# Two transformer-like blocks on one core: order of ropes, stores, norm turns and rotation tables, and where the bias sums are made

## The reference, cut to what matters

```python
xn = layernorm(x)                                    # layer 0
s = attention(xn, 32 heads of 16, rope, causal) @ out_w + out_b
g = silu((silu(xn @ W_gate.T) * (xn @ W_up.T)) @ W_down.T)
x = x + s * g
xn = layernorm(x)                                    # layer 1
h = xn @ Win.T + bin                                 # the "chain", 64 features
for l in range(4):
    y = silu(layernorm(h) * ln1_w[l] + ln1_b[l])
    h = h + sc_lin[l] * Re(complex recurrence of y)  # h_t = p * h_{t-1} + y_t
    y = layernorm(h) * ln2_w[l] + ln2_b[l]
    h = h + silu(y @ W1[l].T + b1[l]) @ W2[l].T + b2[l]
s = (layernorm(h) * lnl_w + lnl_b) @ Wout.T + bout
g = silu(octonion_ffn(xn, ternary(w_gate), ternary(w_up), ternary(w_down)))
x = x + s * g
```

## Time and profile before

| | |
|---|---|
| timed runs | 674.81 us median (671.32, 674.81, 674.85) |
| profiled execution | 678.76 us, its span 677.0 us |
| busy share of the span | PE 92%, DVE 55%, POOL 54%, ACT 41% |
| mean granted PE clock | 0.975 of full speed |
| DMA | 83.24 MB, 123 GB/s mean |

### The profile page before, as it was taken

The page is one execution under the profiler, slowest core; times in us unless marked ns, Lnnn a source line. Parts: engine busy times, 40 slices in busy tenths (PEclk is TensorE's granted clock), DMA queues, the critical chain, the costliest instruction groups (busy, mean ns, idle before and its releaser), DMA issues.

```text
span 677.0 us, 9849 instructions
## 1 busy us (share of the span) xinstructions
PE 621.6 (92%) x3372; PEld 428.2 (63%) x3372; DVE 375.6 (55%) x916; ACT 276.1 (41%) x439; POOL 368.9 (54%) x591
## 2 busy tenths in 40 slices
PE   2978899999999997879999999999999978999996
PEld 2856565666567785546656665677887545757654
DVE  4949668666245592765775653358645240426165
ACT  3514455555634522244555555343122332232323
POOL 4767656555333744865565545347841486730264
PEclk9999999999999999898999999999799987999999
DMA  8687856654312326787575544724500000000002
GB/s 283 185 282 223 254 140 178 179 133 101 119 47 78 88 78 179 208 282 206 127 217 135 132 100 155 274 70 148 187 0 1 1 0 1 0 1 0 1 32 93
DMA packets 59889, 83.24 MB, mean 123 GB/s; under 512 B 17840, under 2 KB 26288, under 8 KB 59840
## 3 DMA queue, kind: packets, MB, share of 16 engines
q1 hardware_dynamic: 56192, 71.35, 36.7%
q10 hardware_dynamic: 3648, 11.27, 4.5%
HBM read 64.78 MB, written 26.99 MB: 136 GB/s over the span
## 4 chain that ended last, share of the span: by engine, by line
PE 72%; DVE 9%; DMA 6%; POOL 5%; issue 3%; ACT 2%; SPq 2%; ACTq 1%; DVEq 0%; POOLq 0%
PE proj_ps L896 8%; PE ctx_ps L1054 6%; PE proj_ps L898 5%; PE proj_ps L897 5%; PE score_ps L926 4%; PE proj_ps L1102 3%; PE proj_ps L1103 3%; PE scoreT_ps L935 3%; DMA rows<-rows_lo 3%; PE score_ps L896 2%; PE score_ps L898 2%; PE score_ps L897 2%; PE scoreT_ps L896 2%; PE scoreT_ps L898 2%; PE scoreT_ps L897 2%
## 5 line engine op out<-in xcount | busy, mean ns | idle before, releaser
L723 POOL TENSOR_TENSOR w_lo<-raw,w_hi 128x512 fp32r<-128x512 f32 x98 | 131.1, 1342 | 71.8 <-ACT w_hi L1253 65.2
L1432 DVE CUSTOM_DVE_ANT_0 score_ps<-score_ps,causal 128x512 f32<-128x512 f32 (+3 forms) x256 | 120.0, 517 | 67.7 <-PE score_ps L926 67.2
L1300 ACT ACTIVATE probs_T<-scoreT_ps 128x1024 f32<-128x1024 f32 (+1 forms) x96 | 84.8, 884 | 83.4 <-PE scoreT_ps L935 82.7
L896 PE MATMUL proj_ps<-xn_hi,w_hi 128*128 128x512 f32 x224 | 101.0, 451 | 5.1 <-DVE gate_silu L1471 2.7
L897 PE MATMUL proj_ps<-xn_hi,w_lo 128*128 128x512 f32 x224 | 89.2, 398 | 0.0
L898 PE MATMUL proj_ps<-xn_lo,w_hi 128*128 128x512 f32 x224 | 89.1, 398 | 0.0
L721 POOL TENSOR_SCALAR w_hi<-raw 128x512 fp32r<-128x512 f32 x50 | 31.1, 621 | 59.2 <-PE proj_ps L898 44.2
L896 PEld LDWEIGHTS proj_ps<-xn_hi,w_hi 128*128 128x128 f32 x224 | 42.5, 190 | 30.4 <-issue 13.5
L926 PE MATMUL score_ps<-k_st,q_st 50*128 50x512 f32 (+3 forms) x256 | 45.1, 389 | 13.8 <-DVE row_max L1432 8.4
L926 PEld LDWEIGHTS score_ps<-k_st,q_st 50*128 50x128 f32 x256 | 21.9, 186 | 54.9 <-issue 28.0
L757 POOL TENSOR_SCALAR_AFFINE_SELECT probs_T<-probs_T 128x256 f32<-128x256 f32 x128 | 50.5, 415 | 10.9 <-ACT probs_T L1300 10.9
(11 more groups left out here) (301 smaller groups left out, 1318.0 us busy)
## 6 DMA issues: line engine op xcount, KB each, us to landing
raw<-w SPq DMA_DIRECT2D x98, 256.0 KB, 2.9
rows<-rows_hi SPq DMA_DIRECT2D x32, 256.0 KB, 3.9
arranged<-tern SPq DMA_DIRECT2D x96, 85.0 KB
q_st<-rows SPq DMA_DIRECT2D x32, 200.0 KB
k_st<-rows SPq DMA_DIRECT2D x32, 200.0 KB
rows<-rows_lo SPq DMA_DIRECT2D x16, 256.0 KB, 4.3
gate_w<-arranged ACTq DMA_DIRECT2D x4, 704.0 KB, 7.1
up_w<-arranged ACTq DMA_DIRECT2D x4, 704.0 KB, 8.0
```

The lines of the kernel that those rows point to most:

```text
L723: nc.gpsimd.tensor_tensor(w_lo[n % SPLIT][:, :], raw[n % RAW][:, :], F32(w_hi[n % SPLIT][:, :]), ALU.subtract).then_inc(unit_ready, 1)
L896: nc.tensor.matmul(acc, lh, rh, start=first, stop=False)
L1300: nc.scalar.activation(probs_T[gp % 4][:, c:c + 2 * w].rearrange("p (h c) -> p h c", h=2), scoreT_ps[:, :, 0:w], ACT.Exp, scale=0.25).then ...
L1432: m = nc.vector.tensor_tensor_reduce(out=block, in0=block, in1=causal[:, S - w:], scale=1.0, scalar=-3e38, op0=ALU.add, op1=ALU.max, accum ...
```

## The change

- Table l lies in buffer l % 3 instead of l % 2. Table 2 enters `todo` at spread(0) and table 3 at conv(2), and a doubling is put only beside an item for whose successor four further on (`AHEAD`) no `hsL` is made. Table 2 waits until the input projection is done, table 3 for layer 0's recurrence. By the list, table 2 is then built beside items 24 to 38 (before: 38 to 52) and table 3 beside items 62 to 76 (before: 60 to 74).
- The running sums of bin and b2 are made by five small POOL operations ahead of table 0, and one product of five columns centres them. W1 times ln2_b is a product and a reduction on DVE in `chain_weights`, on two tensors that SP loads with `winR`.
- DVE does the four rope calls of the next batch between products and residual sums.
- At the head of a batch SP loads 12 units instead of 10, writes the rotated rows after load 9 instead of ahead of it, and reads stack 0 after load 11.
- The six stores of ternary weights are issued by SP in slot 1 of batch 0.
- X is stored tile by tile in slots 24 to 27 of batch 1, and x loaded over it in slots 32 to 35.
- The norm turns 0 and 1 stay in slot 60, and 2 and 3 go to slot 61, on PE, ACT and DVE.

```diff
@@ -142,6 +142,10 @@
+def turns_in(s):
+    return {NORM_TURN: (0, 1), NORM_TURN + 1: (2, 3)}.get(s, ())
+
+
 def turn_order():
@@ -150,9 +154,8 @@
             at["max", max_in(s)] = len(at)
-        if s == NORM_TURN:
-            for kc in range(KC):
-                at["xn", kc] = len(at)
+        for kc in turns_in(s):
+            at["xn", kc] = len(at)
         if s == LAST_DOWN:
@@ -176,7 +179,7 @@
 HI_BY_ACT = FILL + 3
-RAW_HEAD = 10
+RAW_HEAD = 12
 RAW, SPLIT = 4, 5
@@ -187,6 +190,7 @@
+X_OUT, X_BACK = (24, 25, 26, 27), (32, 33, 34, 35)
 W_GATE, W_UP, W_DOWN = range(3)
@@ -353,7 +358,7 @@
     w2T = sb("w2T", [P, DEPTH, 2, C1], f32, offset=o_pt + 22528 + 4096)
-    rotation = [sb(f"rotation{n}", [P, 2, S], f32, offset=o_ctx + 4096 * n) for n in range(2)]
+    rotation = [sb(f"rotation{n}", [P, 2, S], f32, offset=(o_ctx, o_ctx + 4096, o_work + 18432)[n]) for n in range(3)]
     xm_hi = sb("xm_hi", [P, KC, S], f32r, offset=o_v)
@@ -668,11 +678,16 @@
                         write_edges(0)
-                    if u == 8:
+                    if u == 9:
                         write_rows(b, Q_UNIT[0])
                         write_rows(b, K_UNIT[0])
-                        read_rows(b, 0)
+                read_rows(b, 0)
                 for s in range(SCORE_SLOTS + 1):
+                    if b == 0 and s == 1:
+                        for w in range(3):
+                            sp.wait_ge(wp_ready, w + 1)
+                            for x, src in enumerate((tern_pos[w], tern_neg[w])):
+                                sp.dma_start(tern_d[w][x].rearrange("(p n) -> p n", p=P), F32(src[:, :])).then_inc(tern_stored, 16)
                     for u in written_in(s):
@@ -685,19 +700,22 @@
                         sp.dma_start(*copies.pop(0)).then_inc(arranged, 16)
-                    if b == 1 and s == 2:
-                        sp.wait_ge(combined, 2 * NT)
-                        sp.dma_start(x2_d[0].rearrange("t p e -> p t e"), X[:, :, :]).then_inc(x2_stored, 16)
-                    if b == 1 and s == 6:
-                        sp.wait_ge(x2_stored, 16)
-                        for t in range(NT):
-                            sp.dma_start(X[:, t, :], x_dram[1, t]).then_inc(x_in[t], 16)
+                    if b == 1 and s in X_OUT:
+                        if s == X_OUT[0]:
+                            sp.wait_ge(combined, 2 * NT)
+                        sp.dma_start(x2_d[0, X_OUT.index(s)], X[:, X_OUT.index(s), :]).then_inc(x2_stored, 16)
+                    if b == 1 and s in X_BACK:
+                        if s == X_BACK[0]:
+                            sp.wait_ge(x2_stored, 16 * NT)
+                        sp.dma_start(X[:, X_BACK.index(s), :], x_dram[1, X_BACK.index(s)]).then_inc(x_in[X_BACK.index(s)], 16)
                 for u in range(U_DOWN + RAW, UNITS + RAW):
...
             sp.dma_start(winR[:, :, :], A["win"]).then_inc(win_in, 16)
+            sp.dma_start(w1rows[:, :, :, :], A["w1rows"]).then_inc(beta_in, 16)
+            sp.dma_start(beta_rows[:, :, :], A["ln2_b"].partition_broadcast(P)).then_inc(beta_in, 16)
             sp.wait_ge(combined, 2 * NT * B)
@@ -830,13 +848,15 @@
-                if l >= 2:
-                    pool.wait_ge(conv_done, l - 1)
-                nc.gpsimd.tensor_scalar(rotation[l % 2][:, :, 0], polar_v[:, 4:6, l], 1.0, 0.0, mult, add).then_inc(tab_step, 1)
+                if l == 2:
+                    pool.wait_ge(centred, 1)
+                if l >= 3:
+                    pool.wait_ge(conv_done, l - 2)
+                nc.gpsimd.tensor_scalar(rotation[l % 3][:, :, 0], polar_v[:, 4:6, l], 1.0, 0.0, mult, add).then_inc(tab_step, 1)
...
-                m, T = 1 << e, rotation[l % 2]
+                m, T = 1 << e, rotation[l % 3]
                 base = l * (1 + 4 * 9) + 1 + 4 * e
@@ -845,6 +865,12 @@
+            for l in range(DEPTH + 1):
+                if l == 0:
+                    nc.gpsimd.tensor_scalar(b2sum[:, 0:1], vec[:, V_BIN:V_BIN + 1], 1.0, 0.0, mult, add).then_inc(summed, 1)
+                else:
+                    pool.wait_ge(summed, l)
+                    nc.gpsimd.tensor_tensor(b2sum[:, l:l + 1], b2sum[:, l - 1:l], vec[:, V_B2 + l - 1:V_B2 + l], add).then_inc(summed, 1)
             pool.wait_ge(turned, use(B - 1, ("ctxf", KC - 1)) + 1)
@@ -870,15 +896,15 @@
                                                 sub).then_inc(hs1_ready, 1)
-                    if todo and chain not in ("proj", "conv", "mlpout", "var"):
+                    if todo and nxt and nxt[0] == "hid" and chain not in ("proj", "conv", "mlpout", "var"):
                         l, e = todo.pop(0)
...
                     nc.gpsimd.tensor_tensor(inv_std[:, :], var_eps[:, :], half[:, :], ALU.pow).then_inc(rs_ready, 1)
-                elif step[0] == "conv" and step[1] // 2 + 2 < DEPTH:
-                    l = step[1] // 2 + 2
+                elif step in (("spread", 0), ("conv", 2)):
+                    l = 2 if step[0] == "spread" else 3
                     todo += [(l, -1)] + [(l, e) for e in range(9)]
@@ -1056,9 +1082,9 @@
                             m.then_inc(pv_done, 1)
-                    if s == NORM_TURN:
+                    if turns_in(s):
                         pe.wait_ge(proj_free, JOBS * (b + 1))
-                        norm_turn(b + 1)
+                        norm_turn(b + 1, turns_in(s))
@@ -1128,19 +1154,12 @@
                     if step[1] == 1:
-                        pe.wait_ge(biases_made, 2)
+                        pe.wait_ge(biases_made, 1)
                     norm_turn(3, [step[1]])
...
-                    pe.wait_ge(small1_in, 64)
-                    for l in range(DEPTH):
-                        for fc in range(2):
-                            m = nc.tensor.matmul(small_ps[:, 8 + 2 * l + fc:9 + 2 * l + fc], w1T[0:64, l, fc * P:(fc + 1) * P],
-                                                 vec[0:64, V_LN2 + 4 + l:V_LN2 + 5 + l], start=True, stop=True)
-                    for l in range(DEPTH + 1):
-                        v = V_B2 + l - 1 if l else V_BIN
-                        m = nc.tensor.matmul(small_ps[:, 16 + l:17 + DEPTH], centre_m[:, :], vec[:, v:v + 1].broadcast_to([P, DEPTH + 1 - l]),
-                                             start=l == 0, stop=True, skip_group_check=l > 0)
+                    pe.wait_ge(summed, DEPTH + 1)
+                    m = nc.tensor.matmul(small_ps[:, 16:17 + DEPTH], centre_m[:, :], b2sum[:, :], start=True, stop=True)
                     m.then_inc(biases_done, 1)
@@ -1284,9 +1303,6 @@
                         nc.scalar.activation(tern_pos[w][:, :], F32(tern_neg[w][:, :]), ACT.Copy, scale=-1.0).then_inc(wp_ready, 1)
-                        act.wait_ge(wp_ready, w + 1)
-                        for x, src in enumerate((tern_pos[w], tern_neg[w])):
-                            act.dma_start(tern_d[w][x].rearrange("(p n) -> p n", p=P), F32(src[:, :])).then_inc(tern_stored, 16)
                 for s in range(SLOTS):
@@ -1328,10 +1344,9 @@
                         if b:
-                            act.wait_ge(x2_stored, 16)
+                            act.wait_ge(x2_stored, 16 * NT)
                         act.dma_start(x_next[:, :, :], (x2_d[0] if b else x_dram[1]).rearrange("t p e -> p t e")).then_inc(xb_in, 16)
-                    if s == NORM_TURN:
-                        norm_hi(b + 1)
+                    norm_hi(b + 1, turns_in(s))
                     if b == B - 1 and s == SCORE_SLOTS:
@@ -1498,6 +1513,12 @@
+            def first_ropes(b):
+
+                for u in (Q_UNIT[0], K_UNIT[0]):
+                    rope_first(b, u)
+                    rope_second(b, u)
+
             norm_stats(0)
@@ -1506,11 +1527,7 @@
                     dve.wait_ge(rope_in, 48)
-                rope_first(b, Q_UNIT[0])
-                rope_second(b, Q_UNIT[0])
-                rope_first(b, K_UNIT[0])
-                rope_second(b, K_UNIT[0])
-                if b == 0:
+                    first_ropes(0)
                     dve.wait_ge(const_in, 48)
@@ -1562,8 +1579,7 @@
                         norm_rows(b + 1)
-                    if s == NORM_TURN:
-                        norm_lo(b + 1)
+                    norm_lo(b + 1, turns_in(s))
                     if s == LAST_DOWN:
@@ -1590,6 +1606,8 @@
                     nc.vector.tensor_tensor(gate4[b][i][:, :], gate4[b][i][:, :], out_ps[x], ALU.mult).then_inc(combined, 1)
+                if b < B - 1:
+                    first_ropes(b + 1)
                 for x, i in enumerate(OUT_TILES):
@@ -1619,14 +1637,19 @@
                 nc.vector.tensor_tensor(w2, w2, w2_mean[:, :].unsqueeze(2).broadcast_to([P, 2 * DEPTH, C1]), ALU.subtract).then_inc(weights_step, 1)
-                dve.wait_ge(biases_done, 1)
+                dve.wait_ge(beta_in, 32)
+                nc.vector.tensor_tensor(w1beta[:, :, :, :], w1rows[:, :, :, :], beta_rows[:, :, :].unsqueeze(2).broadcast_to([P, DEPTH, 2, C1]),
```

(6 more changed lines are left out.)

18 lines of the change are left out of this document (13 added, 5 removed).

## The result

The changed kernel takes 646.07 us (median of 4 runs, 645.64 to 647.47), the kernel before 674.54 us (median of 4, 671.32 to 674.85). The ratio is 0.9592, 95% interval 0.9559 to 0.9625. The forecast was 641 us, range 636 to 651. The profiled execution took 646.0 us (span 644.1 us); the forecast for it was 644.9.

A forecast was written before the change was run, and what follows sets the result against it. TensorE, busy 92% of the span, was taken as the bound, plus its waits and low-clock stretches. Terms 2.8 + 10.0 + 4.2 + 5.8 + 11.1 = 33.9 us gave 644.9 profiled, 641 us timed, range 636 to 651.

The forecast's parts named there:

- the tables: Third rotation buffer, tables ahead: 12.2 us gained in layer 1's first half, less 0.2 and 0.9, 11.1 us in sum.
- the bias sums: Bias step: 3.2 us of small matmuls on TensorE and 2.6 us of low clock after them go, 5.8 us.
- Start of batch 0: Tern stores leave ScalarE's queue for SP's, so PE's wait on unit 6's gate product goes: 2.8 us.
- its own condition for being wrong: Start of batch 0: the prediction is wrong if slot 6 waits for stacks or stores.
- The second rival: Start of batch 0 is bound by transfers, stores ahead of stacks and exponential: 4.0 us worse, 645; chance 0.09.
- Boundary: Between the batches: earlier ropes, new load order and moved X transfers let batch 1 start like batch 0: 10.0 us.
- Norm turns: Turns split over two slots, once in each batch: the bank wait goes, 2.08 us twice, 4.2 us.
- The 3.2: Bias step: the part of the gain from small matmuls removed from PE, 3.2 us.
- The 0.2 of layer 0: Table 2 built in layer 0 makes the power op 0.7 late; PE loses nothing to 0.2 us.
- the 0.9 of layer 2: Two more doublings ahead of the second power op make it 1.75 late against 0.85 slack: 0.9 us lost.
- The lock rule: VectorE operations with both inputs in SBUF shut GpSimd's reads out; layer 0's scan chain is not slowed, sum stays 33.9.
- From the profiled run to the median: Whole kernel: profiled run before stood 3.95 us above the timed median, so 644.9 became 641 us.

The follow-up runs named there:

- The two repeats: Changed kernel run again unchanged: 648.28 us, ratio 0.9583, profiled 648.56; kernel before run again unchanged: 677.64 us, profiled 678.65.

## Why the prediction was right, and what in it was not

The median lay in the range and the sum for the profiled execution was 33.9 us against 32.8 (678.76 to 646.0). That closeness is in part luck: the first profile of before is 1.1 us above the median of its twelve later runs, and that of the changed kernel 2.3 us below the median of its five. The two repeats give 30.1 us by their profiles (678.65 to 648.56), and the timed ratios 27.5 and 28.2. So the sum was 4 to 6 us too large, mostly in the tables and the bias sums. By its steps:

- **Start of batch 0, 2.8.** Right in size as far as can be told: 3.0 between the two first profiles, 2.2 between their repeats, 2.8 by undoing it alone, while the start by itself varies by 3.5 us. But its own condition for being wrong came true: slot 6 waits for the stacks, 1.1 to 2.7 us in all eight profiles with the stores in slot 1 ahead of them. The second rival was right in its place and wrong in its price. The step that failed is the landing time: I let stores, stacks and some 0.25 MB of weights go at 329 GB/s and put the stacks at 53.8 us; they landed at 57. Of the 3.2 us, 2.0 are there before the stacks are issued: the stores began at 43.96 instead of 42.9 and took 4.5 us to issue instead of 3.5, so the stack read went out at 48.49 instead of 46.5. From 44 to 57 us the engines carried 287 GB/s, 3.7 MB in all, so there was also more on the way, at a lower rate. Slot 6 waited 2.5 us where I had none, not the 4.0 us of the rival. The rule of the Trainium skill that I weighed (DMA: Bandwidth & Descriptors, Queues, rings and completion order), that a DMA engine takes the descriptors of a ring in order, agrees with the runs: with the stores in front the stacks are 2.5 us late, with the stacks in front the stores are, 3.1 us.
- **Boundary, 10.0.** Measured from the end of unit 8 to the first product: 43.8 to 33.65, 10.1. Undone alone, X costs 5.3 and the ropes 1.5 to 2.0 by the profiles (3.4 and 2.3 by the timed ratios); the load order was not tried alone. I had X at 3.1 of late rows and 1.7 of clock; the sum was right, while the late rows act through ScalarE's copy as well.
- **Norm turns, 4.2.** About 4 us by the stages.
- **Bias sums, 5.8.** 6 us between the first profiles (8.0 less 1.9 to 2.1 of norm turns), 5 with the second profile of before, 4.4 by undoing them. The 3.2 was too large: start to start the small matmuls take 3.54 us in the first profile of before, where the clock fell 1.1 us before their end, but 3.01 in its repeat and in the run with them undone. The low clock behind them is in all three profiles, and its length is not fixed.
- **Tables, 11.1.** 9.4 us between the profiles, 8.5 with the repeat: the term that was mis-sized. The half of layer 1 was put at 15.8 us because layer 0's is. But in layer 1 PE's filler is down items, for which GpSimd makes hsL, and layer 0's is hid items, for which it makes nothing. With the tables gone hsL remains, and it meets the scans: 17.83. The prediction had no term for this overlap; it measured 2.05 us. The 0.2 of layer 0 was 0.0, and the 0.9 of layer 2 was 0.7 (17.60 against 16.92), as a wait on inv_std.
- **The lock rule.** The prediction told it, and used it, one-sidedly: GpSimd shut out, VectorE not slowed. In layer 0 that held: scans of 1.28 us beside GpSimd steps stretched to 1.0 to 1.3 us. In layer 1 both are slowed, scans by 0.45 us and hsL by 0.39 on average. The same section of the Trainium skill (SBUF — State Buffer, Who interferes with whom) calls the ports that the two engines share an exclusive lock and says that issue order decides who blocks. The trace agrees in the main: from 521.0 to 528.3 us in layer 1 the two engines' operations end in turn, VectorE's scans 1.08 us after the hsL that was running when they started. An operation of 0.2 us, as GpSimd's in layer 0, can hold VectorE up by little, one of 0.73 us by more. A full block for the whole instruction would make that 1.28 us, so some 0.2 us of each overlap.
- **From the profiled run to the median.** The forecast took 3.95 us off because the profile of before stood so far above its median. This is what made 641 of 644.9. Against the two first profiles it looks like the larger part of the 5 us by which the median was missed; against the repeats the sum that was too large weighs as much. 49 later runs of the kernel before (673.2 to 679.9) put it near 677, and the profile of the changed kernel lay on its own median. The median of three runs was low; why is not shown. It was no property of profiled runs: in the twelve runs here the profiled execution lies between 1.2 us below and 2.4 us above its median.

By the timed ratios the six single undoings cost 25.5 us together, and the changed kernel's repeat gains 28.2. The 2.7 us between are within the intervals of these ratios and can't be given to the new load order. What stays open: how much that order gives by itself, and what decides whether the first matmuls start at 0.39 or 0.63 us each.

## What to carry to other kernels

Compare equal stretches at full clock, but first check that the filler work in them is the same for the other engines too: a half with another kind of items was not what this half would become. When transfers are moved off a busy engine, look for the stretch in which the DMA engines idle and put them there; turning their order in the queue only moved the wait. And an offset between a profile and a median of three runs is not to be carried over.
